# Who issues the copies of the high rows in a two-stage depthwise convolution: GpSimd in place of SyncE

## The chip, the cores and the metric

One NeuronCore of a Trainium2 chip runs the whole program. The metric is the device time of one execution in microseconds, the median of several runs. The profile is of one further execution.

## What is computed

The input x is 8 images of 384 channels of 128 x 128 numbers in float32. Two layers follow each other, and each adds to x a depthwise convolution of a group-normalised x:

```
def _gn(v, G=32, eps=1e-5):
    g = v.reshape(B_, G, C_ // G, H_, W_)
    m = jnp.mean(g, axis=(2, 3, 4), keepdims=True)
    s = jnp.var(g, axis=(2, 3, 4), keepdims=True)
    return ((g - m) / jnp.sqrt(s + eps)).reshape(v.shape)

# layer 0: 3 x 3 taps per channel, padding 1
x = x + _L0_conv_ref(_gn(x), L0_conv_k)
# layer 1: 7 x 7 taps per channel, padding 3, taps averaged over four rotations
x = x + _L1_conv_ref(_gn(x), L1_conv_weight)
```

A group is 12 channels of one image. The second layer's statistics are of the first layer's result, so both layers of a group are needed in order.

## The kernel before

**Tiling.** Image rows lie on the 128 partitions. A chunk n is 4 channels of 4 images (a tile of 128 x 2048 float32 numbers in X), three chunks make a unit (12 channels, one group of each of 4 images), and there are 192 chunks. Every engine walks the same slots t = -5, -4, ...; in slot t it does its share of several chunks at different stages: statistics of chunk t+4, normalising of chunk t+1 for the first convolution, the first convolution of chunk t, normalising of chunk t-3 for the second convolution, the second convolution of chunk t-4, and the last addition and the store of chunk t-5.

**Numbers in two parts.** Both convolutions are matrix products with a band matrix in float16. Each normalised number is split into a high part (rounded to float16) and a low part (what is left): for the first convolution in H1, for the second in H2, which has two buffers, q = n % 2. The high part of H2 is written by GpSimd (high_parts2, four instructions at L635, one per image), the low part by VectorE (L475). The low part of H1 is written by GpSimd (low_parts1, four at L643) from Z, which ScalarE writes (L554).

**The blocks of the second convolution.** TensorE works on four bands of 32 output rows. For each band it wants its window of 36 to 39 input rows on fixed partitions of the tile BT, high and low rows below each other. Twelve DMAs per chunk copy rows from H2 to BT (SBUF to SBUF): gather_high issues four (L235), of 36, 39, 39 and 36 rows of 4256 bytes, and gather_low issues eight (L245 and L247). VectorE then copies the high rows once more inside BT (L508), and waits for the high gathers before it. TensorE's second convolution (L743) waits for that copy and for the low gathers.

**Queues.** Each engine runs its instructions in the order in which they are written. SyncE's slot is: every third slot or so the bands (L275, L296), then the four loads of chunk t+6 (L256, 256 KB each), then a wait for the second convolution of chunk t-5 (BT's buffer is free) and for the high parts of chunk t-3, gather_high(t-3), a wait for the low parts of chunk t-3, gather_low(t-3). Stores are issued by ScalarE (L565). GpSimd's slot is: high_parts2(t-3), then low_parts1(t+1). VectorE's slot is: finish (ten tiny instructions ending at L442 that turn sums into a scale and a bias; once per unit for each layer, so in slots t = 0 and t = 2 modulo 3), the last addition of chunk t-5 (L453), the low parts of chunk t-3 (L475), statistics of chunk t+4 (L484), the first layer's addition of chunk t (L502), the copy of chunk t-3 (L508). TensorE's slot is: first convolution of chunk t (L714), second convolution of chunk t-4 (L743), and tiny products that sum statistics (L679, L686). GpSimd writes the high parts of the first chunk of a unit only when finish of layer 2 has ended (L442); this is slot t = 0 modulo 3.

Of the kernel before, what the change touches and what calls it, by code (L numbers as in the profile page):

```python
# [58 lines left out]
def conv_program(nc, x, k1_in, k2_in, out):  # L59
# [18 lines left out]
    with ExitStack() as ctx:  # L78
# [110 lines left out]
        def wait_apart(eng, semaphore, value):  # L189


            eng.wait_ge(semaphore, value)
            if not isinstance(value, int):
                eng.sem_inc(passed, 1)
# [3 lines left out]
        def real(n):  # L198
            return 0 <= n < NCH

        block = ctx.enter_context(nc.Block())


        @block.sync
        def _(sp):
            sp.dma_start(w1_sb, k1_in.rearrange("(g c) o i j -> g (c o i j)", c=GC)).then_inc(taps_loaded[0], 16)
            sp.dma_start(w2_sb, k2_in.rearrange("(g c) o i j -> g (c o i j)", c=GC)).then_inc(taps_loaded[1], 16)

            def cut1(g0, g1):

                sp.dma_start(rows1[g0 * CPU_:g1 * CPU_],
                             bass.AP(v1_all.tensor, g0 * GC * V1 + (Q - 1) * CC * 2 * K1,
                                     [[CC * V1, (g1 - g0) * CPU_], [-CC * 2 * K1, Q], [1, CC * R1]])
                             ).then_inc(rows1_cut[g0 > 0], 16)

            def cut2(g0, g1):

                first = rows2[0:1, g0:g0 + 1, :]
                sp.dma_start(bass.AP(rows2.tensor, first.offset,
                                     [[B2, (g1 - g0) * 2 * GC], [G * 2 * GC * B2, WIN], [1, B2]]),  # L220
                             bass.AP(v2_all.tensor, g0 * 2 * GC * V2 + (WIN - 1) * K2,
                                     [[V2, (g1 - g0) * 2 * GC], [-K2, WIN], [1, B2]])).then_inc(rows2_cut[g0 > 0], 16)

            def window(b):

                top = b * BL - HALO
                lo_row, hi_row = (0, EDGE) if b == 0 else (P - EDGE, P) if b == NB - 1 else (top, top + WIN)
                return lo_row, hi_row, lo_row - top

            def gather_high(n):  # L230

                q = n % 2
                for b in (0, 2, 1, 3):
                    lo_row, hi_row, r0 = window(b)
                    sp.dma_start(BT[r0:r0 + hi_row - lo_row, q, b, :, :],  # L235
                                 H2[lo_row:hi_row, q, 0, :, :]).then_inc(high_gathered[q], 16)

            def gather_low(n):

                q = n % 2  # L240
                for b in (0, 2, 1, 3):
                    lo_row, hi_row, r0 = window(b)
                    at1, at2 = LOW1 + r0, LOW2
                    middle = lo_row + SPLIT - r0
                    sp.dma_start(BT[at1:at1 + middle - lo_row, q, b, :, :],  # L245
                                 H2[lo_row:middle, q, 1, :, :]).then_inc(low_gathered[q], 16)
                    sp.dma_start(BT[at2:at2 + hi_row - middle, q, b, :, :],  # L247
                                 H2[middle:hi_row, q, 1, :, :]).then_inc(low_gathered[q], 16)

            def load(n, at):  # L250

                c, half = n % CPU_, (n // CPU_) % HALVES
                ch0 = (at(n - n % GCH) // GCH) * GC + c * CC
                for img in range(NI):
                    src = x[half * NI + img, bass.ds(ch0, CC), :, :].rearrange("c h w -> h c w")
                    sp.dma_start(xs(n, img), src).then_inc(x_loaded[n % BODY], 16)  # L256

            def slot(t, at):

                n = t + 2  # L260
                if real(n) and n % GCH < CPU_:
                    c = n % CPU_
                    g = at(n - c) // GCH
                    if n >= GCH:
                        if n == GCH:
                            sp.wait_ge(rows1_cut[1], 16)
                        wait_apart(sp, conv1_done, at(n) - CPU_ + 1)
                    elif n == 0:
                        sp.wait_ge(rows1_cut[0], 16)
                        sp.wait_ge(zeroed, 8)  # L270
                    for q in range(P // Q):

                        m0, m1 = max(q * Q - 1, 0), min((q + 1) * Q + 1, P)
                        k0 = (m0 - (q * Q - 1)) * CC * 2 * K1
                        sp.dma_start(BAND1[q * Q:(q + 1) * Q, c, m0 * CC * 2 * K1:m1 * CC * 2 * K1],  # L275
                                     rows1[g * CPU_ + c, :, k0:k0 + (m1 - m0) * CC * 2 * K1]
                                     ).then_inc(band1_loaded[c], 16)

                n = t
                if real(n) and n % GCH == 0:  # L280
                    g = at(n) // GCH
                    half = (n // GCH) % 2
                    if n == 0:
                        sp.wait_ge(prep[1], PREP[1])
                        sp.wait_ge(zeroed, 12)
                        sp.dma_start(v2_all, v2_sb).then_inc(vectors_stored[1], 16)
                        sp.wait_ge(vectors_stored[1], 16)
                        cut2(0, CUT)
                        sp.wait_ge(rows2_cut[0], 16)
                    elif n >= 2 * GCH:  # L290
                        if n == 2 * GCH:
                            sp.wait_ge(rows2_cut[1], (G // CUT - 1) * 16)
                        wait_apart(sp, conv2_done, at(n) - GCH)
                    for to, r0, r1, which in ((0, 0, WIN, 0), (AGAIN, 0, WIN, 1), (LOW1, 0, SPLIT, 0),
                                              (LOW2, SPLIT, WIN, 0)):
                        sp.dma_start(BAND2[to:to + r1 - r0, half, :, :].rearrange("r c k -> r (c k)"),  # L296
                                     rows2[r0:r1, g, which * GC * B2:(which + 1) * GC * B2]
                                     ).then_inc(band2_loaded[half], 16)
                if 0 < t < G // CUT:
                    cut2(t * CUT, (t + 1) * CUT)  # L300

                n = t + AHEAD
                if real(n) and n >= AHEAD - 3:
                    if n // CPU_ == RING - 1:

                        sp.wait_ge(vectors_stored[0], 16)
                        sp.wait_ge(vectors_stored[1], 16)
                        sp.wait_ge(scales_summed, 2)
                    if n >= BODY:
                        wait_apart(sp, stored[n % BODY], (at(n - n % BODY) // BODY) * (16 * NI))  # L310
                    load(n, at)

                n = t - 3
                if real(n):
                    if n < 2:
                        sp.wait_ge(blocks_zeroed, 1)
                    else:
                        wait_apart(sp, conv2_done, at(n) - 1)
                    wait_apart(sp, hi_done[1], NI * at(n) + NI)
                    gather_high(n)  # L320
                    wait_apart(sp, lo_done[1], NI * at(n) + NI)
                    gather_low(n)


            for n in range(AHEAD - 3):
                load(n, lambda m: m)
            sp.wait_ge(prep[0], PREP[0])
            sp.dma_start(v1_all, v1_sb).then_inc(vectors_stored[0], 16)
            sp.wait_ge(vectors_stored[0], 16)
            cut1(0, 1)  # L330
            cut1(1, G)
            walk(sp, slot)
            for place in range(BODY):
                sp.wait_ge(stored[place], NCH // BODY * 16 * NI)
# [272 lines left out]
        def _(pool):  # L607
# [18 lines left out]
            def high_parts2(n, at):  # L626
# [7 lines left out]
                for img in range(NI):  # L634
                    g.tensor_scalar(part(H2, n, 0, img, O2, P2), xs(n, img), rb[:, 0, img:img + 1],  # L635
                                    rb[:, 1, img:img + 1], ALU.mult, ALU.add).then_inc(hi_done[1], 1)

            def low_parts1(n, at):

                for img in range(NI):  # L640
                    wait_apart(pool, normed[0], NI * at(n) + img + 1)
                    wait_apart(pool, hi_done[0], NI * at(n) + img + 1)
                    g.tensor_tensor(part(H1, n, 1, img, O1, P1), Z[:, img, :].rearrange("p (c w) -> p c w", c=CC),  # L643
                                    part(H1, n, 0, img, O1, P1), ALU.subtract).then_inc(lo_done[0], 1)

            def slot(t, at):
                if real(t - 3):
                    high_parts2(t - 3, at)
                if real(t + 1):
                    low_parts1(t + 1, at)  # L650
                if t == 1:
# [117 lines left out]
```

## Time and profile before

| | |
|---|---|
| median of 3 runs | 3432.22 us (3426.28 to 3436.23) |
| the profiled execution, its own time | 3437.14 us |
| its span in the profile | 3435.3 us |
| mean granted clock of TensorE | 0.953 of full speed |
| busy: TensorE / VectorE / ScalarE / GpSimd | 85% / 80% / 63% / 47% of the span |
| share of the 16 DMA engines' time on packets | 8 tenths in nearly every slice |

In the rows further down PE is TensorE's matrix product, PEld its weight load, DVE is VectorE, ACT ScalarE, POOL GpSimd, SP SyncE. A name with q (SPq, ACTq) is the engine's own queue: time in which it issues DMAs, which isn't counted as busy. "A <- B" in a table of waits says that A's engine stood idle until B had ended.

### The profile page before, as it was taken

How to read it: one execution, taken by the hardware profiler on the slowest of the kernel's cores; microseconds unless marked ns; L12 is line 12 of the kernel's file. 1: busy time of each engine (PE TensorE's matmuls, PEld its weight loads, DVE VectorE, ACT ScalarE, POOL GpSimd, SP SyncE). 2: the span in 40 equal slices, each digit the busy share in tenths (PEclk: the TensorE clock that was granted, in tenths of full speed). 3: DMA queues.
4: the chain of work that ended last, by engine and by line, in shares of the span. 5: the costliest groups of instructions: out<-in, count | busy, mean ns of one | idle time of the engine just before them, and what ended most of it. 6: DMA issues, size and time to landing. Idle time of an engine off the chain costs nothing.

```text
span 3435.3 us, 76363 instructions
## 1 busy us (share of the span) xinstructions
PE 2912.2 (85%) x28676; PEld 1839.2 (54%) x28676; DVE 2756.5 (80%) x5180; ACT 2176.9 (63%) x3969; POOL 1613.0 (47%) x1553
## 2 busy tenths in 40 slices
PE   0468888989898889888888889898989989898995
PEld 0245555555555555555555555555555555555553
DVE  3548888888788888888878888888888888788885
ACT  1346666666676667666666666666666766676672
POOL 3324544544455445454444445444445544454552
PEclk9888999999999999999999999999999999999998
DMA  2698888888888888888888888888878888888866
GB/s 88 174 222 216 210 212 215 218 208 213 219 214 222 213 215 210 209 211 211 224 214 205 209 215 217 216 217 214 215 208 218 215 215 215 211 210 219 214 171 156
DMA packets 955769, 712.41 MB, mean 207 GB/s; under 512 B 92166, under 2 KB 893958, under 8 KB 955334
## 3 DMA queue, kind: packets, MB, share of 16 engines
q1 hardware_dynamic: 549894, 506.13, 58.8%
q10 hardware_dynamic: 405504, 201.38, 20.9%
q8 instruction: 227, 3.72, 0.5%
q14 instruction: 144, 1.18, 0.1%
HBM read 259.73 MB, written 220.81 MB: 140 GB/s over the span
## 4 chain that ended last, share of the span: by engine, by line
SPq 46%; DVE 26%; DMA 11%; issue 8%; POOL 5%; PE 2%; ACT 1%; ACTq 0%; DVEq 0%; POOLq 0%
SPq L235 15%; DMA BT<-H 10%; SPq L256 9%; SPq L245 9%; SPq L247 8%; DVE BT L508 5%; POOL H L635 5%; DVE H L475 4%; DVE X L502 4%; SPq L275 4%; DVE BN L484 4%; DVE X L453 2%; SPq L296 1%; PE PS L743 1%; PE PS L714 1%
## 5 line engine op out<-in xcount | busy, mean ns | idle before, releaser
L714 PE MATMUL PS<-H,BAND 128*128 128x512 f16 x6912 | 1617.4, 394 | 108.6 <-DMA BAND<-rows 72.3
L643 POOL TENSOR_TENSOR H<-Z,H 128x512 f16<-128x512 f32 x768 | 864.5, 1128 | 1422.0 <-ACT Z L554 1421.6
L743 PE MATMUL PS<-BT,BAND 118*32 118x512 f16 x21504 | 1273.4, 395 | 172.7 <-DVE X L453 140.6
L714 PEld LDWEIGHTS PS<-H,BAND 128*128 128x128 f16 x6912 | 1026.7, 152 | 654.1 <-issue 127.7
L743 PEld LDWEIGHTS PS<-BT,BAND 118*32 118x32 f16 x21504 | 792.1, 132 | 643.2 <-issue 307.9
L551 ACT ACTIVATE H<-X,RB 128x512 f16<-128x512 f32 x768 | 618.8, 806 | 493.4 <-DVE H L475 482.0
L635 POOL TENSOR_SCALAR H<-X,RB 128x512 f16<-128x512 f32 x768 | 721.9, 954 | 353.0 <-DVE RB L442 344.5
L508 DVE COPY BT<-BT 39x8512 f16<-39x8512 f16 x192 | 464.4, 2419 | 457.2 <-DMA BT<-H 455.1
L534 ACT ACTIVATE Z<-X,RB 128x512 f32<-128x512 f32 x768 | 562.2, 804 | 109.0 <-DVE RB L442 83.6
L554 ACT ACTIVATE Z<-X,RB 128x512 f32<-128x512 f32 x768 | 615.7, 802 | 0.0
L577 ACT ACTIVATE DUMP<-X 128x512 bf16<-128x512 f32 x768 | 476.5, 622 | 139.4 <-DVE X L502 139.4
L484 DVE BATCH_NORM_STATS2 BN<-X 128x6 f32<-128x512 f32 x768 | 473.1, 679 | 79.8 <-DMA X<-in_x 79.7
L502 DVE SCALAR_TENSOR_TENSOR X<-PS,SC,X 128x512 f32<-128x512 f32 x768 | 528.4, 744 | 3.8 <-PE PS L714 3.8
L475 DVE TENSOR_TENSOR H<-Z,H 128x512 f16<-128x512 f32 x768 | 516.3, 732 | 13.9 <-POOL H L635 8.1
L453 DVE SCALAR_TENSOR_TENSOR X<-PS,SC,X 128x2048 f32<-128x2048 f32 x192 | 451.3, 2351 | 17.9 <-PE PS L743 11.4
L569 ACT ACTIVATE TMP<-TMP 128x4 f32<-128x4 f32 x128 | 26.3, 205 | 489.2 <-DVE TMP L434 489.2
L577 ACT ACTIVATION_READ_ACCUMULATOR DUMP<-X 128x1 f32 x768 | 143.9, 187 | 0.0
L679 PE MATMUL PS<-SS,ONES 128*128 128x24 f32 x128 | 27.6, 296 | 117.5 <-ACT DUMP L577 117.5
L686 PE MATMUL PS<-MQ,ONES 128*128 128x8 f32 x128 | 25.2, 269 | 93.1 <-DVE X L502 84.4
L679 PEld LDWEIGHTS PS<-SS,ONES 128*128 128x128 f32 x128 | 20.8, 204 | 146.9 <-ACT DUMP L577 145.3
L686 PEld LDWEIGHTS PS<-MQ,ONES 128*128 128x128 f32 x128 | 20.9, 205 | 119.9 <-issue 119.9
L502 DVE DVE_READ_ACCUMULATOR X<-PS,SC,X 128x1 f32 x768 | 63.2, 82 | 0.0
(47 smaller groups left out, 418.7 us busy)
## 6 DMA issues: line engine op xcount, KB each, us to landing
X<-in_x SPq DMA_DIRECT2D x768, 256.0 KB, 4.1
out_y<-X ACTq DMA_DIRECT2D x768, 256.0 KB, 5.3
BT<-H SPq DMA_DIRECT2D x384, 162.1 KB
BT<-H SPq DMA_DIRECT2D x384, 149.6 KB
BT<-H SPq DMA_DIRECT2D x576, 99.8 KB
BT<-H SPq DMA_DIRECT2D x384, 62.3 KB
BT<-H SPq DMA_DIRECT2D x192, 83.1 KB
rows<-v_all SPq DMA_DIRECT2D x8, 1638.0 KB, 10.9
```

Of the source, the lines that this page charges most:

```text
L475: v.tensor_tensor(part(H2, n, 1, img, O2, P2), Z[:, img, :].rearrange("p (c w) -> p c w", c=CC), part(H2, n, 0, img, O2, P2), ALU.subtract ...
L484: v.bn_stats(BN[:, c, img, :], xs(n, img)).then_inc(bn_done, 1)
L502: v.scalar_tensor_tensor(xs(n, img), PA[:, :, img * W:(img + 1) * W], SC[:, 0, bass.ds(g, 1)], xs(n, img), ALU.mult, ALU.add, accum_out=SS ...
L508: v.tensor_copy(BT[AGAIN:AGAIN + WIN, n % 2, :, :, :].rearrange("p b c l -> p (b c l)"), BT[0:WIN, n % 2, :, :, :].rearrange("p b c l -> p ...
L534: nc.scalar.activation(Z[:, img, :].rearrange("p (c w) -> p c w", c=CC), xs(n, img), ACT.Identity, bias=rb[:, 1, img:img + 1], scale=rb[:, ...
L551: nc.scalar.activation(part(H1, n, 0, img, O1, P1), xs(n, img), ACT.Identity, bias=rb[:, 1, img:img + 1], scale=rb[:, 0, img:img + 1]).the ...
L554: nc.scalar.activation(Z[:, img, :].rearrange("p (c w) -> p c w", c=CC), xs(n, img), ACT.Identity, bias=rb[:, 1, img:img + 1], scale=rb[:, ...
L577: nc.scalar.activation(DUMP[:, img % 2].rearrange("p (c w) -> p c w", c=CC), xs(n, img), ACT.Square, accum_out=SS[:, n % CPU_, img, 1:2]). ...
L635: g.tensor_scalar(part(H2, n, 0, img, O2, P2), xs(n, img), rb[:, 0, img:img + 1], rb[:, 1, img:img + 1], ALU.mult, ALU.add).then_inc(hi_do ...
L643: g.tensor_tensor(part(H1, n, 1, img, O1, P1), Z[:, img, :].rearrange("p (c w) -> p c w", c=CC), part(H1, n, 0, img, O1, P1), ALU.subtract ...
L714: last = mm(PA[:, ch, :], band[:, j, ws, :], data[:, :, O1 - 1 + j:O1 - 1 + j + W], start=k == 0, stop=k == 3 * K1 - 1)
L743: last = mm(banks2(n)[b * BL:(b + 1) * BL, ch, :], band[:, j, :], rows, start=j == 0, stop=j == K2 - 1, tile_position=(0, b * BL))
```

## The change

The four high gathers of a chunk leave SyncE's program and are issued by GpSimd between its high parts of that chunk and its low parts of chunk t+1. The two waits go with them: for the second convolution of chunk t-5, and for the high parts, which GpSimd has itself written just before. SyncE keeps its wait for the second convolution ahead of the low gathers. Rows, sizes, targets and semaphores of the DMAs are the same, and so is VectorE's, ScalarE's and TensorE's program.

```diff
@@ SyncE, slot @@
                     else:
                         wait_apart(sp, conv2_done, at(n) - 1)
-                    wait_apart(sp, hi_done[1], NI * at(n) + NI)
-                    gather_high(n)
                     wait_apart(sp, lo_done[1], NI * at(n) + NI)
                     gather_low(n)
@@ GpSimd @@
+            def gather_high(n):
+
+                q = n % 2
+                if n < 2:
+                    pool.wait_ge(blocks_zeroed, 1)
+                else:
+                    pool.wait_ge(conv2_done, n - 1)
+                pool.wait_ge(hi_done[1], NI * n + NI)
+                for b in (0, 2, 1, 3):
+                    lo_row, hi_row, r0 = window(b)
+                    pool.dma_start(BT[r0:r0 + hi_row - lo_row, q, b, :, :],
+                                   H2[lo_row:hi_row, q, 0, :, :]).then_inc(high_gathered[q], 16)
@@ GpSimd, slot @@
                 if real(t - 3):
                     high_parts2(t - 3, at)
+                    gather_high(t - 3)
                 if real(t + 1):
                     low_parts1(t + 1, at)
```

GpSimd's program in the steady part, before. lo_done, hi_done and the others in brackets are the semaphores that an instruction waits for; a 2 behind a name is the second layer.

```order
31 L635 TENSOR_SCALAR H<-X,RB 128x4x128 [waits low_gathered1,high_gathered1,fin2]
32 L635 TENSOR_SCALAR H<-X,RB 128x4x128 x3
33 L643 TENSOR_TENSOR H<-Z,H 128x4x128 [waits hi_done1,normed1] x4
34 L635 TENSOR_SCALAR H<-X,RB 128x4x128 [waits low_gathered0,high_gathered0,fin2]
35 L635 TENSOR_SCALAR H<-X,RB 128x4x128 x3
36 L643 TENSOR_TENSOR H<-Z,H 128x4x128 [waits hi_done1,normed1] x4
```

The same place of GpSimd's program after the change (L635 is now L625, L643 is L646).

```order
40 L625 TENSOR_SCALAR H<-X,RB 128x4x128 [waits low_gathered1,high_gathered1,fin2]
41 L625 TENSOR_SCALAR H<-X,RB 128x4x128 x3
42 L638 DMA BT<-H 36x2128 [waits hi_done2,conv2_done]
43 L638 DMA BT<-H 39x2128 x2
44 L638 DMA BT<-H 36x2128
45 L646 TENSOR_TENSOR H<-Z,H 128x4x128 [waits hi_done1,normed1] x4
```

Four DMAs and a wait for TensorE's second convolution now stand between the high parts and the low parts of every slot.

SyncE's program in one slot, before.

```order
307 L256 DMA X<-in_x 128x4x128 [waits stored3]
308 L256 DMA X<-in_x 128x4x128 x3
309 L235 DMA BT<-H 36x2128 [waits hi_done2,conv2_done]
310 L235 DMA BT<-H 39x2128 x2
311 L235 DMA BT<-H 36x2128
312 L245 DMA BT<-H 20x2128 [waits lo_done2]
313 L247 DMA BT<-H 16x2128
314 L245 DMA BT<-H 24x2128
```

SyncE's program in one slot after the change (L256 is now L248, L245 is L237, L247 is L239).

```order
306 L248 DMA X<-in_x 128x4x128 [waits stored7]
307 L248 DMA X<-in_x 128x4x128 x3
308 L237 DMA BT<-H 20x2128 [waits lo_done2,conv2_done]
309 L239 DMA BT<-H 16x2128
310 L237 DMA BT<-H 24x2128
```

The loads are now followed by the low gathers, and the wait for the second convolution stands ahead of these.

## Rows read from the trace of the kernel before

**Rows 1.** The page, chain that ended last: shares of the span by engine.
```profile
SPq 46%; DVE 26%; DMA 11%; issue 8%; POOL 5%; PE 2%; ACT 1%; ACTq 0%; DVEq 0%; POOLq 0%
```
**Rows 2.** Waits of the whole span: engine, line, releaser, us in total, times, longest.
```profile
POOL H L643 <- ACT Z L554: 1421.6, 703, 72.2
...
DVE BT L508 <- DMA BT<-H: 455.1, 128, 16.1
```
**Rows 3.** Waits of SyncE's own queue, the two longest.
```profile
SPq L192 <- POOL H L635: 161.9, 51, 7.4
SPq L245 <- DVE H L475: 125.2, 63, 5.7
```
**Rows 4.** The page, costliest groups: busy us, mean ns of one, idle before.
```profile
L643 POOL TENSOR_TENSOR H<-Z,H 128x512 f16<-128x512 f32 x768 | 864.5, 1128 | 1422.0 <-ACT Z L554 1421.6
...
L635 POOL TENSOR_SCALAR H<-X,RB 128x512 f16<-128x512 f32 x768 | 721.9, 954 | 353.0 <-DVE RB L442 344.5
...
L484 DVE BATCH_NORM_STATS2 BN<-X 128x6 f32<-128x512 f32 x768 | 473.1, 679 | 79.8 <-DMA X<-in_x 79.7
...
L475 DVE TENSOR_TENSOR H<-Z,H 128x512 f16<-128x512 f32 x768 | 516.3, 732 | 13.9 <-POOL H L635 8.1
...
L453 DVE SCALAR_TENSOR_TENSOR X<-PS,SC,X 128x2048 f32<-128x2048 f32 x192 | 451.3, 2351 | 17.9 <-PE PS L743 11.4
```
**Rows 5.** Line L508: ns min/median/max, first and last start in us.
```profile
L508 DVE COPY BT<-BT x192: 2370/2372/3051, 186.9 to 3409.4; 39x8512 f16<-39x8512 f16 x192
```
**Rows 6.** Four stretches of six slots: busy us (x instructions) per engine, clock, DMA.
```profile
1598.00:1700.00 102.00, 92.70 (x904) 57.64 (x903) 86.41 (x166) 69.33 (x126) 49.50 (x48) 0.96 0.83 212
...
sum 411.00, PE 369.50 PEld 232.93 DVE 344.25 ACT 274.89 POOL 197.72; mean PE 92.37 PEld 58.23 DVE 86.06 ACT 68.72 POOL 49.43
```
**Rows 7.** Timeline of a slot t = 0 modulo 3: start us, us, engine.
```profile
1714.77 4.05 POOL L635 TENSOR_SCALAR H<-X,RB 128x512 f16<-128x512 f32 x4 [4.66 <-DVE RB L442]
...
1718.89 4.99 SPq L235 DMA_DIRECT2D BT<-H  x4
...
1719.64 6.34 PE L743 MATMUL PS<-BT,BAND 118*32 118x512 f16 x112
...
1723.60 1.09 POOL L643 TENSOR_TENSOR H<-Z,H 128x512 f16<-128x512 f32 x1 [0.32 <-ACT Z L554]
...
1724.94 0.08 DVE L502 DVE_READ_ACCUMULATOR X<-PS,SC,X 128x1 f32 x1
...
1725.91 8.07 PE L714 MATMUL PS<-H,BAND 128*128 128x512 f16 x36
...
1727.47 2.45 DVE L508 COPY BT<-BT 39x8512 f16<-39x8512 f16 x1 [2.45 <-DMA BT<-H]
```
**Rows 8.** Timeline of the next slot, t = 1 modulo 3.
```profile
1724.67 3.02 POOL L635 TENSOR_SCALAR H<-X,RB 128x512 f16<-128x512 f32 x4
...
1734.60 1.09 POOL L643 TENSOR_TENSOR H<-Z,H 128x512 f16<-128x512 f32 x1 [6.91 <-ACT Z L554]
...
1735.49 5.89 SPq L235 DMA_DIRECT2D BT<-H  x4
...
1745.91 2.37 DVE L508 COPY BT<-BT 39x8512 f16<-39x8512 f16 x1 [4.49 <-DMA BT<-H]
```
**Rows 9.** Issue time of one DMA, ns min/median/max: high gathers, stores.
```profile
L235 SPq DMA_DIRECT2D BT<-H x768: 714/806/2999, 177.4 to 3402.0; - x192
...
L565 ACTq DMA_DIRECT2D out_y<-X x768: 378/518/2805, 215.7 to 3431.4; - x192
```
**Rows 10.** Pieces of the chain that ended last, window 1760 to 1803: the landing.
```profile
1775.30 8.35 DMA BT<-H
```
**Rows 11.** Timeline of another slot: GpSimd's high parts beside VectorE's copy.
```profile
2303.03 5.22 POOL L635 TENSOR_SCALAR H<-X,RB 128x512 f16<-128x512 f32 x4
...
2304.57 2.38 DVE L508 COPY BT<-BT 39x8512 f16<-39x8512 f16 x1
...
2334.59 3.01 POOL L635 TENSOR_SCALAR H<-X,RB 128x512 f16<-128x512 f32 x4
```

More of the change, by code:

```diff
@@ L199, in real, with window @@
             return 0 <= n < NCH
+        def window(b):
+            top = b * BL - HALO
+            lo_row, hi_row = (0, EDGE) if b == 0 else (P - EDGE, P) if b == NB - 1 else (top, top + WIN)
+            return lo_row, hi_row, lo_row - top
         block = ctx.enter_context(nc.Block())
@@ L222, in cut2 @@
                                      [[V2, (g1 - g0) * 2 * GC], [-K2, WIN], [1, B2]])).then_inc(rows2_cut[g0 > 0], 16)
[L224 to L236, printed above, removed]
             def gather_low(n):
```

## The prediction

> **What bounds the kernel now.** I read the chain that ended last first. 46% of it is SyncE's queue and 11% the landing of the copies into BT, while VectorE has 26% and TensorE 2% [rows 1]. So the time is set by how soon SyncE gets its copies out. The waits say where that is felt: VectorE's copy L508 stands idle for the high gathers for 455.1 us in 128 of 192 slots, its longest wait [rows 2]. SyncE itself hardly waits: 161.9 us for the high parts and 125.2 us for the low parts [rows 3]. It is behind with issuing, not waiting for data.
>
> Next, what a slot costs. L508 starts first at 186.9 and last at 3409.4 us, 192 times [rows 5], so a slot is 3222.5 / 191 = 16.87 us and three slots (a unit) 50.6 us. In four stretches of six slots (102.75 us on average) TensorE is busy 92.37, VectorE 86.06 and GpSimd 49.43 us [rows 6]. VectorE's 102.75 are thus 86.06 of work, 455.1 / 32 = 14.2 of waiting for high gathers, and 2.5 of all else. If the gathers came in time, VectorE would need 88.5 us for six slots and TensorE would need its own 92.4 or a little less. TensorE's room is the narrower of the two.
>
> Where the gathers are late: in a slot t = 1 modulo 3, GpSimd had the high parts ready at 1724.67 + 3.02 = 1727.7, and TensorE had ended the convolution that frees BT at 1719.64 + 6.34 = 1726.0, but SyncE, still at its low gathers, bands and loads, issued the high gathers from 1735.49 to 1741.4, and VectorE's copy began at 1745.91 after 4.49 us of idle time [rows 7, 8]. Eight microseconds pass with the data ready. In the slot t = 0 there is no such gap: the high parts end at 1718.82 and SyncE issues at 1718.89 [rows 7]. There the order itself is the limit, and VectorE waits 2.45 us.
>
> **What goes, what moves.** From SyncE: four issues per slot, the stretch of 4.99 us in one slot and 5.89 us in the next [rows 7, 8], about 5.4 of 16.87 us. SyncE's low gathers, loads and bands stay, so it has about 5 us of air per slot and is no bound any more. The low gathers wait only for VectorE's low parts then and start about as early as before or earlier. That is priced at nothing. TensorE wants them one slot later, after the next first convolution of 8.07 us [rows 7].
>
> To GpSimd: four issues per slot, 768 in all, two waits, and behind them low_parts1 (L643). Those who wait for that are TensorE's first convolution (L714) and, for the tile Z, ScalarE. No row shows a DMA issued by GpSimd with an access pattern. The nearest rows: a store issued by ScalarE takes 0.38 us at least, SyncE's high gather 0.81 us in the median and 3.00 us at most [rows 9], GpSimd's own instructions 0.95 and 1.13 us [rows 4]. Nothing excludes less than 0.38 us of GpSimd's time; below nothing it can't be, since the instructions are added. I take 1.1 us, the price of one instruction of this engine on this side of the bounds, so 4.4 us for four. The ends for the range are 0.4 and 3.0 us, or 1.6 and 12 us per slot.
>
> Is GpSimd free for it? It works (721.9 + 864.5) / 192 = 8.26 us per slot [rows 4] and waits for ScalarE 1421.6 us in total [rows 2]. With 4.4 it is at 12.7 of 16.87. On the whole it fits. By place: in slot t = 1 it would issue from 1727.7 to 1732.1, and it first needs Z at 1734.60, after 6.91 us of idle time [rows 8]: covered, and 2.5 us are left if the slot comes no earlier. The wait for the second convolution costs nothing there (1726.0 against 1727.7). In slot t = 0 nothing covers it: issues from 1718.9 to 1723.3, then four low parts of 1.09 us, so the last ends at 1727.7 and not at 1723.60 + 1.09 = 1724.7 [rows 7]. TensorE begins L714 at 1725.91, right behind its L743, so it would stand for 1.8 us there.
>
> **When the high rows land.** In slot t = 0, SyncE's last issue ended at 1723.88 and the copy began at 1727.47 with nothing ahead in the queue: 3.6 us for the landing [rows 7]. With GpSimd the last issue ends at 1723.3, the landing is at 1726.9, and VectorE has ended L502 at 1725.02: it waits 1.9 us in place of 2.45. So slot t = 0 gains almost nothing. In slot t = 1 the landing is at 1732.1 + 3.6 = 1735.7. VectorE has then ended the preceding copy at 1726.9 + 2.4 = 1729.3 and has (451.3 + 516.3 + 473.1) / 192 = 7.5 us of L453, L475 and L484 ahead [rows 4], which brings it to 1736.8, and L502 besides: no wait. The same holds for t = 2, where the tiny instructions of finish are added. The worst landing of before, 8.35 us [rows 10], was behind four loads in the same queue of SyncE, which the changed order removes.
>
> **Sum.** 3435.3 us of span, less all 455.1 us of VectorE's wait, plus 64 slots t = 0 with 1.9 us (121.6): 3101.8 us. TensorE's stall of 1.8 us lies in the same slot beside VectorE's 1.9 us: L714 then ends at 1727.7 + 8.07 = 1735.8, and VectorE, whose next use of it is L502, wants it at 1736.8 (above). So it isn't added. The cross-check is TensorE: 32 stretches of 92.37 us and 3435.3 - 32 x 101.2 = 196 us at both ends make 3152 us if its busy time doesn't shrink at all. But it shrinks, since its 92.37 us hold time at a granted clock of 0.96 and matrix products drawn out by waits; one pair in the trace takes 8.07 + 6.34 = 14.41 us [rows 7], so six pairs take 86.5 us. TensorE lies between 2964 and 3152 us and doesn't forbid 3102. The profiled execution's own time is 1.8 us over its span and 4.9 us over the median: 3101.8 + 1.8 - 4.9 = 3098.7, said as **3100 us**.
>
> **A rule that speaks against the change.** When VectorE's copy L508 runs (2304.57 to 2306.95), GpSimd's four high parts take 5.22 us and not 3.01 [rows 11]: GpSimd is held for 2.2 us by the copy. The same hold could hit the issues, or the issues could hold the copy. The Trainium skill, "SBUF — State Buffer", in its warning that VectorE blocks DMA, says that a DMA issued from GpSimd has its descriptors written by GpSimd's cores, which a VectorE operation using both of its ports locks out, and advises SyncE's or ScalarE's queue. The trace agrees for GpSimd's arithmetic; no run here shows it for a DMA.
>
> **Rivals.** (a) The hold becomes the new wait. The mechanism: the copy L508 of the preceding slot or the next falls on the four issues, and each time 2.4 us are lost on GpSimd, and then on the high rows. In the forecast's places the issues stand 4 us and more behind the copy, which speaks against it; but in slots t = 1 and 2 GpSimd runs as soon as it can, near the copy. If one slot in three loses 2.4 us: 64 x 2.4 = 154 us, 3255 us. (b) The landing is slower. Gathers from GpSimd compete with loads and stores at a DMA share of 0.83 [rows 6], and would be at 0.92 in the shorter time. With a landing of 6 us in place of 3.6, slot t = 0 waits 4.3 us and the others nothing or little: 64 x 2.4 = 154 more and some 40 for the others, 3295 us. (c) Slower than before: GpSimd becomes the bound. Its slot has 16.87 - 8.26 = 8.6 us of room, which four issues of 2.15 us use up; that is the point from which it decides, within the bounds of 0.4 and 3.0 us. At 2.5 us each a slot is 8.26 + 10 = 18.3 us, and 191 of them with the 212.8 us outside [rows 5] make 3700 us. Against it speaks that only the longest of SyncE's issues are that long. (d) The issue is cheap, 0.4 us: slot t = 0 has its rows at 1724.1 and no wait, so the sum is 3435.3 - 455.1 = 2980 us; TensorE then binds near 3000. (e) The change doesn't do what it says, because something else is late in VectorE's place, for example the low gathers or TensorE's sums, and most of the gain goes: 3420 us, within 0.3% or near it.
>
> **How the numbers follow.** Forecast (3040 to 3180) 0.50; (a) 0.10; (b) 0.12; (c) 0.12; (d) 0.08; (e) 0.08. Measurements of this kernel tell no more than 0.3% (10 us) apart from no change. Faster takes the forecast, (a), (b), (d) and half of (e), slower takes (c) and a little of (e): faster 0.83, same 0.04, slower 0.13. For the range I leave out (c) and part of (e) above and a bit of (d) below: 2990 to 3400 us.
>
> **What would show it.** Right: GpSimd's DMA issues take about 1.1 us each; VectorE's wait for BT falls from 455.1 to about 120 us and stays in slots t = 0 alone; SyncE's queue is no longer the largest part of the chain, with VectorE, TensorE and GpSimd in its place; low parts in slot t = 0 end some 3 us later, with a wait of TensorE's L714 or weight load for them. Wrong: issues of 2 us and more with GpSimd near 100% (c); issues that are long only where they meet L508 (a); more than 5 us between the last issue and the landing (b); a wait for the low gathers at L743 or a TensorE busy time that stays near 92 us per six slots (e).

## The result, and the profile after

| | before | after |
|---|---|---|
| median | 3429.25 us | 3324.17 us |
| ratio, 95% interval | | 0.9685 [0.9664, 0.9706] |
| span of the profiled execution | 3435.3 us | 3322.5 us |
| VectorE's wait for the high rows | 455.1 us, 128 times | 292.2 us, 69 times |

The change is faster, by 3.1% and not by the 9.6% that was forecast. The measured time lies inside the stated range of 2990 to 3400 us, but the gain is a third of what the sum gave.

First the page of the changed kernel: the chain that ended last by engine and the group of the new instructions (beside [rows 1, 4]).

```profile
DVE 49%; DMA 13%; issue 13%; POOL 10%; ACT 5%; PE 5%; SPq 4%; ACTq 1%; DVEq 0%; POOLq 0%
...
L646 POOL TENSOR_TENSOR H<-Z,H 128x512 f16<-128x512 f32 x768 | 835.7, 1099 | 677.5 <-ACT Z L544 676.5
...
L625 POOL TENSOR_SCALAR H<-X,RB 128x512 f16<-128x512 f32 x768 | 798.7, 1048 | 341.3 <-DVE RB L432 318.6
...
L638 POOL DMA_DIRECT2D BT<-H x768 | 465.9, 612 | 142.7 <-POOL H L625 101.8
```

SyncE's queue has gone from 46% of the chain [rows 1] to 4%. GpSimd pays 0.61 us for an issue, a good half of the 1.1 us assumed. The landing of the copies still has 13%, as before (11%).

VectorE's waits after (beside [rows 2]):

```profile
DVE BT L498 <- DMA BT<-H: 292.2, 69, 7.9
...
DVE ST L418 <- PE PS L690: 27.4, 6, 12.4
DVE ST L420 <- PE PS L683: 15.6, 7, 8.3
```

And a slot t = 0 of the changed kernel (beside [rows 7]; L625 are GpSimd's high parts, L638 its gathers, L237 SyncE's low gathers, L646 its low parts, L492 the first layer's addition, L718 TensorE's next first convolution, L498 the copy):

```profile
1708.60 4.05 POOL L625 TENSOR_SCALAR H<-X,RB 128x512 f16<-128x512 f32 x4 [4.65 <-DVE RB L432]
...
1713.22 2.05 POOL L638 DMA_DIRECT2D BT<-H  x4 [0.56 <-POOL H L625]
...
1713.87 0.78 SPq L237 DMA_DIRECT2D BT<-H  x1
...
1715.29 4.23 POOL L646 TENSOR_TENSOR H<-Z,H 128x512 f16<-128x512 f32 x4
...
1718.78 0.07 DVE L492 DVE_READ_ACCUMULATOR X<-PS,SC,X 128x1 f32 x1
...
1719.75 8.08 PE L718 MATMUL PS<-H,BAND 128*128 128x512 f16 x36
...
1723.76 2.37 DVE L498 COPY BT<-BT 39x8512 f16<-39x8512 f16 x1 [4.90 <-DMA BT<-H]
```

GpSimd is through with issuing at 1715.27. The rows are there 8.5 us later. The line of the gathers in this slot says the same for each DMA:

```profile
L638 POOL DMA_DIRECT2D BT<-H x4: 505/506/558, 1713.2 to 1714.8; - x4
...
DMA to landing us min/median/max: 6.2/7.7/9.0
```

What the DMA engines do meanwhile is in the queues' shares, from 1715 to 1716 us and then from 1713 to 1724 us (q0 is GpSimd's queue, q1 SyncE's, q10 ScalarE's; packets, MB, share of 16 engines, where packets in flight at once can make it more than 100%):

```profile
q1 hardware_dynamic: 412, 0.20, 75.1%
q10 hardware_dynamic: 237, 0.12, 41.5%
```
```profile
q1 hardware_dynamic: 2030, 1.34, 48.3%
q10 hardware_dynamic: 2087, 1.04, 33.6%
q0 software_dynamic: 256, 0.64, 21.4%
```

Nearly three microseconds behind the first issue (1713.22) not one packet of GpSimd's queue has run; loads and stores fill the engines. The first packet with rows starts at 1717.89 in this slot. Over the 11 us all three queues together take 103% of the engines' time.

To compare the kernels I took, in the 58 units of chunks 12 to 185, the mean times between rows of the timeline: how long VectorE stands before its copy in slots t = 0, 1, 2, and in slots t = 0 the time from the start of the first high gather's issue to the copy, with the part in which the four are issued.

| kernel | wait in t = 0 / 1 / 2 | first issue to copy | of it issuing |
|---|---|---|---|
| before | 4.06 / 1.93 / 0.43 us | 9.70 us | 4.87 us |
| after | 4.38 / 0.01 / 0.00 us | 9.85 us | 2.06 us |

So the change removes the waits of the slots t = 1 and 2 wholly and of the slots t = 0 not at all. The issuing there got 2.8 us shorter and the end came no sooner.

The trace has every DMA packet with its size, and a packet of a high row is one of 4256 bytes. Counted over the same units, 47 of the 150 rows had started by the end of SyncE's last issue before the change, and 4 by the end of GpSimd's last issue after it.

### The profile page after: what moved, and what is told of

Read it like the earlier page. It is cut to its first block, busy times and chain, and to the rows that moved or that the text cites. A ratio compares the mean times of both kernels' runs of the same rounds, so it can differ in the third digit from the quotient of the medians.

```text
span 3322.5 us, 76555 instructions
## 1 busy us (share of the span) xinstructions
PE 2873.4 (86%) x28676; PEld 1813.7 (55%) x28676; DVE 2768.8 (83%) x5180; ACT 2176.0 (65%) x3969; POOL 2127.9 (64%) x2321
## 4 chain that ended last, share of the span: by engine, by line
DVE 49%; DMA 13%; issue 13%; POOL 10%; ACT 5%; PE 5%; SPq 4%; ACTq 1%; DVEq 0%; POOLq 0%
DMA BT<-H 12%; DVE X L492 9%; DVE H L465 9%; DVE BN L474 8%; DVE BT L498 8%; POOL H L625 7%; DVE X L443 4%; PE PS L747 3%; SPq L248 2%; PE PS L718 2%; POOL BT L638 2%; POOL H L646 2%; ACT Z L524 2%; ACT H L541 1%; DVE TMP L423 1%
## 5 line engine op out<-in xcount | busy, mean ns | idle before, releaser
L718 PE MATMUL PS<-H,BAND 128*128 128x512 f16 x6912 | 1609.2, 393 | 90.3 <-DMA BAND<-rows 72.2
L718 PEld LDWEIGHTS PS<-H,BAND 128*128 128x128 f16 x6912 | 1026.2, 151 | 628.5 <-issue 125.1
L747 PE MATMUL PS<-BT,BAND 118*32 118x512 f16 x21504 | 1245.8, 389 | 95.6 <-DMA BT<-H 40.8
L646 POOL TENSOR_TENSOR H<-Z,H 128x512 f16<-128x512 f32 x768 | 835.7, 1099 | 677.5 <-ACT Z L544 676.5
L747 PEld LDWEIGHTS PS<-BT,BAND 118*32 118x32 f16 x21504 | 767.3, 131 | 560.1 <-issue 200.3
L625 POOL TENSOR_SCALAR H<-X,RB 128x512 f16<-128x512 f32 x768 | 798.7, 1048 | 341.3 <-DVE RB L432 318.6
L498 DVE COPY BT<-BT 39x8512 f16<-39x8512 f16 x192 | 465.0, 2422 | 296.1 <-DMA BT<-H 292.2
L638 POOL DMA_DIRECT2D BT<-H x768 | 465.9, 612 | 142.7 <-POOL H L625 101.8
L492 DVE SCALAR_TENSOR_TENSOR X<-PS,SC,X 128x512 f32<-128x512 f32 x768 | 528.2, 742 | 4.2 <-PE PS L718 4.1
L465 DVE TENSOR_TENSOR H<-Z,H 128x512 f16<-128x512 f32 x768 | 505.8, 717 | 15.9 <-POOL H L625 11.0
L683 PE MATMUL PS<-SS,ONES 128*128 128x24 f32 x128 | 26.4, 286 | 93.5 <-ACT DUMP L567 93.5
```

Source lines behind the costliest of these rows:

```text
L465: v.tensor_tensor(part(H2, n, 1, img, O2, P2), Z[:, img, :].rearrange("p (c w) -> p c w", c=CC), part(H2, n, 0, img, O2, P2), ALU.subtract ...
L492: v.scalar_tensor_tensor(xs(n, img), PA[:, :, img * W:(img + 1) * W], SC[:, 0, bass.ds(g, 1)], xs(n, img), ALU.mult, ALU.add, accum_out=SS ...
L498: v.tensor_copy(BT[AGAIN:AGAIN + WIN, n % 2, :, :, :].rearrange("p b c l -> p (b c l)"), BT[0:WIN, n % 2, :, :, :].rearrange("p b c l -> p ...
L718: last = mm(PA[:, ch, :], band[:, j, ws, :], data[:, :, O1 - 1 + j:O1 - 1 + j + W], start=k == 0, stop=k == 3 * K1 - 1)
L747: last = mm(banks2(n)[b * BL:(b + 1) * BL, ch, :], band[:, j, :], rows, start=j == 0, stop=j == K2 - 1, tile_position=(0, b * BL))
```

## The experiments

All kernels stand beside runs of the kernel before on the same chip; the ratio is to these. The changed kernel is at 0.9685. VectorE's wait in slots t = 0 is a mean of the 58 units.

**Loads behind the low gathers.** Is it the four loads, issued just ahead of the high rows, that hold them up?

```diff
 def slot(t, at):            # SyncE
-                    load(n, at)          # n = t + AHEAD, with its wait
...
                     gather_low(n)
+                    load(n, at)          # n = t + AHEAD, with its wait
```

> The changed kernel with one edit: SyncE issues the four loads of chunk t+6 behind the low gathers of chunk t-3 and not ahead of them. In the changed kernel GpSimd's issues in a slot t = 0 modulo 3 end at 1715.3 us and the rows land at 1723.8, and no packet of GpSimd's queue runs before 1717, while loads and stores fill the engines. Theory A (loads ahead hold the high rows up): the landing in slots t = 0 falls from 8.5 to 4 to 5 us, VectorE's wait for BT from 292 us to 80 to 130 us, the time to 3150 to 3220 us. Theory B (the low gathers, now in flight at the same time, hold them up): they come earlier here, so the wait stays at 290 us or grows, 3320 to 3350 us. Theory C (GpSimd's DMAs start late in themselves): the wait stays near 290 us, 3310 to 3330 us.

Measured: 3300.48 us, ratio 0.9623 [0.9606, 0.9641]. The wait in slots t = 0 is 4.18 us, in total 280.8 us. It is a gain of 0.6% over the changed kernel, but theory A asked for a wait of a third. The loads' place isn't the cause. The time also lies below the bounds of theories B and C (3310 us at least), so none of the three had it.

**Low gathers after the high rows have landed.** Is it the low rows, which now travel at the same time?

```diff
                     wait_apart(sp, lo_done[1], NI * at(n) + NI)
+                    sp.wait_ge(high_gathered[n % 2], (n // 2 + 1) * HIGH_LANDED)
                     gather_low(n)
```

> The changed kernel with one edit: SyncE waits, ahead of the low gathers of a chunk, until the high gathers of that chunk have landed. Theory A (loads hold the high rows up): first packets no earlier, landing a little shorter since the low rows are out of the way, wait of VectorE 230 to 290 us; the low rows come some 4 us later in slots t = 0, with a wait of TensorE's second convolution for them; 3310 to 3370 us. Theory B (the low gathers hold them up): landing in slots t = 0 falls to 4 to 5 us, VectorE's wait to 80 to 130 us, time 3180 to 3260 us. Theory C (late in themselves): wait 290 us, 3330 to 3370 us.

Measured: 3516.1 us, ratio 1.0251 [1.023, 1.0271]. The wait in slots t = 0 is 3.98 us, in total 278.0: theory B is out as well. The time is far above all expectations. VectorE's second wait says where it comes from:

```profile
DVE BT L499 <- DMA BT<-H: 278.0, 68, 8.6
DVE ST L419 <- PE PS L691: 262.0, 63, 12.5
```
```profile
PE PS L748 <- DMA BT<-H: 208.8, 27, 16.6
```

TensorE now waits for the low rows in its second convolution (208.8 us), its sums come late, and VectorE's finish waits 262.0 us for them. TensorE's mean granted clock is 0.924 in this kernel and 0.962 in the changed one, and TensorE has 55% of the chain; how much of the added time is the clock was not separated. The low rows have less slack than the forecast's "one slot later" suggests.

**SyncE issues the high rows, but first.** Nothing on GpSimd; the place in SyncE's slot moves ahead of bands and loads.

```diff
 def slot(t, at):            # SyncE, kernel before
+                n = t - 3
+                if real(n):
+                    ...
+                    wait_apart(sp, hi_done[1], NI * at(n) + NI)
+                    gather_high(n)
                 n = t + 2
...
-                    wait_apart(sp, hi_done[1], NI * at(n) + NI)
-                    gather_high(n)
```

> The kernel before with one edit: SyncE issues the high gathers at the head of its slot, ahead of bands and loads, and nothing is issued by GpSimd. The issues cost SyncE as much as before, the place is early as in the change. Theory A (what counts is that no load stands ahead of the high rows): VectorE's wait for BT falls from 455 us to under 200 us, and the time to 3200 to 3300 us, at or below the changed kernel. Theory C (it counts that SyncE's queue has less to issue): the time stays within 30 us of 3430 us, since SyncE issues as much as before and the loads and bands now wait behind the high parts. If GpSimd's queue is slow in itself, the landing here is shorter than the 8.5 us of the changed kernel.

Measured: 3447.57 us, ratio 1.0059 [1.0036, 1.0083]: within the 30 us of theory C, slightly slower than before. The waits are 2.42 / 2.78 / 0.98 us: better than before in t = 0, worse in t = 1 and 2. From the first issue to the copy it is 8.60 us, 4.97 of it issuing and 3.63 behind the last issue. So an early place with as much to issue isn't enough. This fits theory C, that SyncE must have less to issue; no run takes issues from SyncE without giving them to another queue. The second thing to read: issuing takes 4.97 us here and 2.06 us on GpSimd, but issue and landing together are 8.60 and 9.85 us. The time behind the last issue is short on SyncE because the copies already run while it issues: 79 of the 150 rows have started by its end.

**A quarter of the loads' bytes.**

```diff
+                    cc = CC if n < BODY else 1
-                    src = x[half * NI + img, bass.ds(ch0, CC), :, :].rearrange("c h w -> h c w")
+                    src = x[half * NI + img, bass.ds(ch0, cc), :, :].rearrange("c h w -> h c w")
...                                              # and as much of the tile is written
```

> The changed kernel, which from chunk 12 on loads one channel in four (a quarter of the bytes of the loads, the same number of DMAs); the other channels are left out and what the chunk's buffer held is used again. Theory A (loads hold the high rows up): landing in slots t = 0 falls to 4 to 5 us, VectorE's wait from 292 to under 120 us, time 3100 to 3200 us. Theory B or C: the wait stays above 220 us and the time above 3250 us.

Measured: 3275.21 us, ratio 0.9549 [0.9521, 0.9577]; wait in slots t = 0 3.52 us, in total 241.2 us. That is in theory B's and C's bounds, but not nothing: the loads' bytes cost 0.9 us of 4.4.

**A quarter of the high rows' own bytes.** Does the landing take long because of a late start or because of the transfer?

```diff
+                    cc = CC if n < 2 else 1
-                    pool.dma_start(BT[r0:r0 + hi_row - lo_row, q, b, :, :],
-                                   H2[lo_row:hi_row, q, 0, :, :]).then_inc(high_gathered[q], 16)
+                    pool.dma_start(BT[r0:r0 + hi_row - lo_row, q, b, 0:cc, :],
+                                   H2[lo_row:hi_row, q, 0, 0:cc, :]).then_inc(high_gathered[q], 16)
```

> The changed kernel, whose high gathers copy one channel of four from chunk 2 on: the same four DMAs and rows, a quarter of the bytes (1064 of 4256 per row); the other channels' high rows are left out. Before this run: moving the loads or the low gathers out of the way left VectorE's wait in slots t = 0 at 4.2 and 4.0 us of 4.4. Theory D (the copies' own transfer takes the time: some 5.5 us from the first to the last packet of GpSimd's queue): the wait in slots t = 0 falls below 1.5 us, in total from 292 to under 100 us, the time to 3080 to 3180 us. Theory E (the start: the first packet comes 2 to 4 us behind the issue, whatever the size): the wait stays at 2.5 us or more in each slot t = 0, over 170 us in total, time 3230 us or more.

Measured: 3171.64 us, ratio 0.9253 [0.9205, 0.9301]; wait in slots t = 0 1.38 us, in total 97.0 us; 6.80 us from the first issue to the copy. Theory D by all three numbers. A remainder of 4.7 us behind the last issue stays with a quarter of the bytes, so a start of some microseconds is in it too. What this run can't tell is why the transfer of the whole rows takes so long: their own bytes alone, or their bytes in the traffic of the others.

**All others at a quarter.** Loads, stores and low gathers with the edit above, the high rows whole.

```diff
+                    cc = CC if n < 2 else 1          # low gathers; n < BODY in load and store
-                    sp.dma_start(BT[at1:at1 + middle - lo_row, q, b, :, :],
-                                 H2[lo_row:middle, q, 1, :, :]).then_inc(low_gathered[q], 16)
+                    sp.dma_start(BT[at1:at1 + middle - lo_row, q, b, 0:cc, :],
+                                 H2[lo_row:middle, q, 1, 0:cc, :]).then_inc(low_gathered[q], 16)
...                                              # the same for the second DMA of the block
```

> The changed kernel with all other large DMAs at a quarter of their bytes: loads and stores one channel in four from chunk 12 on, low gathers one channel of four from chunk 2 on; the rest is left out. The high gathers are whole. Theory F (the traffic as a whole delays them, none of its parts alone): the wait of slots t = 0 falls from 4.4 to under 2 us, in total under 130 us, time 3110 to 3180 us. Theory D (their own transfer) and E (their start): the wait stays above 2.5 us, over 170 us in total, time 3200 us or more.

Measured: 3173.12 us, ratio 0.9258 [0.922, 0.9296]; wait in slots t = 0 1.82 us, in total 136.8 us (the expectation said under 130); 7.00 us from the first issue to the copy. Its waits, and its DMA share in 411 us of the steady part with the changed kernel's behind it (last numbers: clock, share, GB/s):

```profile
DVE BT L500 <- DMA BT<-H: 136.8, 68, 6.4
```
```profile
1598.00:2009.00 411.00, 385.44 (x3933) 244.41 (x3926) 376.57 (x706) 296.19 (x544) 296.74 (x314) 0.99 0.40 100
```
```profile
1598.00:2009.00 411.00, 376.00 (x3791) 239.34 (x3793) 360.97 (x677) 287.93 (x524) 277.89 (x301) 0.98 0.87 222
```

At a share of 0.40 in place of the changed kernel's 0.87 the whole high rows land almost as soon as the quartered ones do with the others' traffic whole. Theory D alone, which asked for a wait of 2.5 us or more, is out. The traffic as a whole, the high rows' own bytes included, is what holds them up: theory F.

**A quarter of the stores' bytes.** Which part of the traffic? The stores are issued in the same microseconds.

```diff
+                cc = CC if n < BODY else 1
-                dst = out[half * NI + img, bass.ds(ch0, CC), :, :].rearrange("c h w -> h c w")
-                act.dma_start(dst, xs(n, img)).then_inc(stored[n % BODY], 16)
+                dst = out[half * NI + img, bass.ds(ch0, cc), :, :].rearrange("c h w -> h c w")
+                act.dma_start(dst, X[:, ring(n), c * CC:c * CC + cc, img, :]).then_inc(stored[n % BODY], 16)
```

> The changed kernel, whose stores write one channel in four from chunk 12 on (same number of DMAs, a quarter of the bytes; the rest of the result isn't written). The stores are issued by ScalarE in the microseconds in which GpSimd issues the high rows in a slot t = 0. Theory F1 (the stores are the part of the traffic that counts): wait of slots t = 0 falls from 4.4 us to below 2.8 us, time 3190 to 3240 us. Theory F2 (only the sum of all traffic counts, each part a little, as with the loads, 3.5 us): wait 3.2 to 3.9 us, time 3250 to 3300 us.

Measured: 3229.68 us, ratio 0.9434 [0.9414, 0.9454]; wait in slots t = 0 2.53 us, in total 200.8 us. Theory F1: the stores alone are worth 1.85 us of 4.38, twice the loads.

**VectorE's copy later.** If the wait can't be shortened, it can be covered. The copy of a unit's first chunk moves into the next slot, behind the last addition, or behind the low parts too.

```diff
 def slot(t, at):            # VectorE
                     add_conv2(t - 5, at)
+                if t % CPU_ == 1:
+                    copy_again(t - 4, at)      # the wait and the copy L498
...
-                    dve.wait_ge(high_gathered[n % 2], ...)
-                    v.tensor_copy(...)
+                if t % CPU_ != 0:
+                    copy_again(t - 3, at)
```

> The changed kernel; VectorE's copy of the first chunk of a unit moves from the end of slot t = 0 behind the last addition (2.35 us) of the next slot, where the wait for the high rows is covered by that addition. If the wait of 4.4 us in 58 of 58 slots t = 0 is time of the whole kernel one for one: 64 x 2.35 = 150 us less, 3165 to 3185 us. If TensorE or something else is the bound behind it: a wait for the addition or the low rows takes its place, and the time stays above 3230 us.

Measured: 3258.17 us, ratio 0.9508 [0.9478, 0.9538]. The wait of the first chunks falls to 0.96 us, in total to 89.0, but the time by 66 us and not by 150.

```profile
DVE X L443 <- PE PS L753: 119.0, 63, 7.0
DVE BT L450 <- DMA BT<-H: 89.0, 58, 7.8
```

203 us of waiting for rows are gone and 111 us of waiting for TensorE's second convolution have come (119.0 against 7.9 in the changed kernel), with 29 us more for GpSimd's high parts (39.6 against 11.0). So the second reading of the expectation holds, in mechanism and in time (above 3230 us): something else binds behind the wait.

**The copy behind the low parts too.** The same edit with the two lines of copy_again(t - 4, at) four instructions further down, behind L465.

> As the run with the copy behind the addition, but the copy stands behind the low parts too (L465, 2.4 us more), so the whole wait of 4.4 us is covered. One for one: 64 x 4.4 = 280 us less, 3045 us, if TensorE's second convolution, which waits for the copy, isn't delayed; it has the first convolution of 8 us to do first. I expect 3060 to 3130 us, since TensorE's busy time alone is some 90 us for six slots of 98. If TensorE binds: 3150 us or more, with its wait for the copy L498 or for the low rows in the list.

Measured: 3327.71 us, ratio 0.9717 [0.9679, 0.9754]: the same as without the edit. No wait for the high rows of first chunks is left (0.05 us), but TensorE's second convolution waits 121.7 us for low rows (40.8 in the changed kernel), VectorE 88.0 us for the second convolution and 93.5 us for its sums. SyncE's queue is back in the chain with 23%. Expected were 3060 to 3130 us; the other case, TensorE, was named with its sign. The profile is of the fastest of its four executions (3301.8 us), so its waits may differ from those of the median.

**The late copy and the loads last.** Both edits as above: the copy behind the addition, the loads behind the low gathers.

> The changed kernel with VectorE's copy of a unit's first chunk behind the next slot's addition (3258 us) and the loads behind the low gathers (that edit alone was 24 us faster than the changed kernel). If the two add up: 3225 to 3245 us. If the loads' place only mattered through the wait that the late copy already covers: 3250 to 3265 us.

Measured: 3239.47 us, ratio 0.9464 [0.9436, 0.9492]. The two add up. It is the fastest kernel here that computes the whole result, 5.4% under the kernel before. TensorE's two convolutions are 29% of its chain.

**The late copy and the stores last.**

```diff
 def slot(t, at):            # ScalarE, on top of the late copy
-                    if real(t - 5):
-                        store(t - 5, img, at)
                 if real(t):
                     square(t, at)
+                for img in range(NI):
+                    if real(t - 5):
+                        store(t - 5, img, at)
```

> The changed kernel with VectorE's copy of a unit's first chunk behind the next slot's addition, and with ScalarE's stores issued behind its squares at the end of its slot, some 8 us later, out of the way of the high rows. Theory F1 (the stores hold the high rows up): landings in slots t = 0 fall from 7.7 to 6 us or less, no wait left for the copy, and 3200 to 3240 us. Theory F2: landings of 7 us and more; the stores come later, so the loads wait for them: 3250 to 3300 us.

Measured: 3269.28 us, ratio 0.9547 [0.9528, 0.9566]. The high rows land 7.09 us behind the last issue on average, against 7.96 with the late copy alone. Landing and time are both in F2's bounds. SyncE's loads wait 511.9 us for the stores, and 70.8 with the late copy alone:

```profile
SPq L248 <- DMA out_y<-X: 511.9, 139, 11.0
```
```profile
SPq L248 <- DMA out_y<-X: 70.8, 46, 4.7
```

Moving the stores moves the traffic, it doesn't take it away. With a quarter of their bytes the landing did fall, as F1 had it there; both results fit the sum of all traffic.

**The late copy in the kernel before.** The edit of VectorE's slot alone; SyncE still issues the high gathers.

> The kernel before, high gathers on SyncE, with the late copy alone. Its wait in slots t = 0 is 4.1 us, about as long as in the changed kernel. If the late copy is worth the same here as in the changed kernel (66 us), 3345 to 3375 us. If SyncE's queue sets the pace of this kernel, so that a wait covered in VectorE comes back as a wait for a later gather: 3400 to 3430 us.

Measured: 3383.93 us, ratio 0.9887 [0.9864, 0.9909]. The late copy is worth 40 us in the kernel before and 66 us in the changed one. The time lies between the two cases of the expectation and in neither. The waits of the three chunks are 0.92 / 3.22 / 0.27 us against 4.06 / 1.93 / 0.43: part of what is covered in the first chunk comes back in the second, where SyncE is late.

## Why the prediction went wrong, by its own steps

**SyncE as the bound, and its relief: right.** Its queue fell from 46% to 4% of the chain. The kernel in which SyncE issued early but as much as before stayed at 1.0059. The waits in slots t = 1 and 2 went to 0.01 and 0.00 us, as said.

**The issue on GpSimd: too dear.** 1.1 us were assumed, 0.61 measured (median 0.505). Rival (c), GpSimd as the bound, needed 2.15 us. This error hid a part of the next one. With the measured 2.06 us for four issues the prediction's own working has the rows at 1718.9 + 2.06 + 3.6 = 1724.6, ahead of the end of L502 at 1725.02, so without a wait: the sum would have been rival (d)'s 2980 us, 120 us further from the result. That the forecast wasn't further off is luck. TensorE's stall for the low parts in slots t = 0, forecast with 1.8 us and not added, doesn't show among its waits: L646 comes right behind the issues and ends at 1719.52, and TensorE begins L718 at 1719.75, when its own second convolution is through.

**The landing in slots t = 0: the term that failed.** The sum put 1.9 us of wait on each of 64 slots, from one row: the last issue of SyncE's ended at 1723.88 and the copy began at 1727.47, 3.6 us [rows 7]. Two errors are in it. One is the sample. That slot waited 2.45 us, the mean of 58 such slots is 4.06, and behind the last issue the mean is 4.83 us and not 3.6. The other is the method. The 3.6 us stood behind an issue stretch of 4.99 us during which the copies already ran: in that slot 79 of the 150 rows had started when the last issue ended. They were taken as a delay that starts with the last issue, and GpSimd's shorter issuing was then expected to bring the end forward. From the first issue to the copy it is 9.70 us before and 9.85 us after, and behind the last issue 7.79 us after the change where 3.6 was put. With the mean of 4.38 in place of 1.9, the sum is 3435.3 - 455.1 + 64 x 4.38 = 3260.5 us. The rest to the span of 3322.5 is 62 us: 12.3 us more VectorE work (2768.8 against 2756.5), 11.9 us of wait for gathers outside this mean (292.2 - 280.3), and 36.7 us more waiting for TensorE's sums (27.4 and 15.6 us against 1.5 and 4.8). The lines of before for these (VectorE's busy time, then its waits for the sums), and VectorE's busy time after:

```profile
PE 2912.2 (85%) x28676; PEld 1839.2 (54%) x28676; DVE 2756.5 (80%) x5180; ACT 2176.9 (63%) x3969; POOL 1613.0 (47%) x1553
```
```profile
DVE ST L430 <- PE PS L679: 4.8, 6, 1.9
...
DVE ST L428 <- PE PS L686: 1.5, 2, 0.7
```
```profile
PE 2873.4 (86%) x28676; PEld 1813.7 (55%) x28676; DVE 2768.8 (83%) x5180; ACT 2176.0 (65%) x3969; POOL 2127.9 (64%) x2321
```

**The rival that came true.** It was (b), slower landing, forecast at 6 us and 3295 us with a chance of 0.12. Its mechanism, gathers that compete with loads and stores at a high DMA share, is shown by the quartered kernels. Its size was too small: 7.8 us behind the last issue on average. Rival (a), the hold between VectorE's copy and GpSimd's issues, wasn't needed for it; it shows, but elsewhere (below).

**The sum itself: right in kind, some 70 us short.** The quartered kernels bring about the wait that was assumed, 1.38 and 1.82 us in place of 1.9, and take 3171.64 and 3173.12 us where 3100 was forecast. So about two thirds of the error of 224 us are the landing, and a third would have stayed with the landing as assumed. That the whole wait comes off one for one was the assumption there. The late copy shows the same: 203 us less waiting for rows brought 66 us, since waits for TensorE's second convolution took their place. The cross-check by TensorE's busy time (2964 to 3152 us) left room for this and wasn't turned into a term.

**Late start or slow transfer: both.** The packets of GpSimd's queue divide the time (means of the 58 units, us): from the start of the first issue to the start of the first packet with rows, and from there to the end of the last packet.

| kernel | to the first packet | first to last packet |
|---|---|---|
| changed | 3.11 | 6.30 |
| loads a quarter | 2.09 | 6.37 |
| stores a quarter | 1.73 | 5.53 |
| all others a quarter | 1.14 | 5.01 |
| high rows a quarter | 3.08 | 2.77 |

So the others' traffic costs 2.0 us at the start and 1.3 us in the transfer, and the high rows' own bytes set most of the rest. The start depends on the others' loads and stores and not on the rows' own size. VectorE's instructions are the same in all five, so a hold by VectorE isn't what delays the start.

**What stays open.** Why the first packet comes later when loads and stores are in flight. A kernel with high gathers alone in flight wasn't run.

## What to carry to other kernels

When DMAs move to another queue, measure from the first issue to the landing, not from the last one: a queue that issues slowly overlaps its issuing with the transfer, and a faster issuer gives nothing where the transfer or the traffic around it sets the end. Moving an issue pays where the old queue is late with it, slot by slot; ask of each slot separately whether the data were ready before the queue was, and take the mean of many such slots, not one. Where a landing can't be hurried, put other work of the waiting engine ahead of its wait, and look at who waits for what now comes later: 2.35 us of cover for a wait of 4.4 us gave 2% here, and 5.4 us of cover (the addition and the four low parts, 3.08 us) gave nothing.

## What the runs showed of the hardware

GpSimd issues a gather of 36 to 39 rows of 4256 bytes in 0.505 us (median), less than SyncE's 0.806 us [rows 9]. Its first issue starts 0.56 us behind its own last high part in the slot shown, where SyncE's started 0.07 us behind it [rows 7]; in all that is 101.8 us of GpSimd's time.

In slots t = 0 the first packet with rows starts 1.14 us behind the start of GpSimd's first issue (1.12 to 1.62) where the DMA share is 0.40, and 3.11 us behind it (1.18 to 5.16) where it is 0.87.

A copy by VectorE does hold up GpSimd's issuing. In this stretch of the changed kernel four issues take 4.20 us and not 2.05, with the copy L498 beside them:

```profile
2798.64 4.20 POOL L638 DMA_DIRECT2D BT<-H  x4 [0.56 <-POOL H L625]
...
2798.87 2.37 DVE L498 COPY BT<-BT 39x8512 f16<-39x8512 f16 x1 [4.47 <-DMA BT<-H]
```

That is 2.15 us more, about one copy, as GpSimd's high parts were held in [rows 11]. It is so over the whole trace: the 60 issues that overlap a copy take 1.73 us on average, the other 708 take 0.52 us and none of them more than 0.72 us. It agrees with the warning of the Trainium skill, "SBUF — State Buffer", section "SBUF: two separate sides", that a VectorE operation on both ports locks out GpSimd's descriptors. That L498 is such an operation isn't shown here; only the time of the hold is. All issues together take 465.9 us and would take 768 x 0.505 = 388: some 78 us more, 74 of them in those 60 issues, on an engine that waits 676.5 us for ScalarE anyway. The hold is there and costs nothing that can be seen: VectorE's waits in slots t = 1 and 2 are 0.01 and 0.00 us.
